# Two-layer graph residual norm on one core: z kept in three h buffers, transposes in other banks, a new order of work on every engine

## The chip, the cores and the metric

The kernel runs on one core of one Trainium2 chip. The metric is the time of one execution on the device, in microseconds; lower is better. The five engines are named PE (TensorE, matmuls; PEld is its loading of weights), DVE (VectorE), ACT (ScalarE), POOL (GpSimd) and SP (SyncE, which here issues all transfers). They run their own instruction streams and meet at semaphores only.

## What is computed

x is 128 batches of 64 nodes with 512 features, fp32. Layer 0 mixes nodes with the squared-by-element adjacency, adds a bias and normalises x plus that. Layer 1 builds two 64 x 64 affinities per batch, from projections z_l and z_g, mixes them, applies them to a value projection, projects again, adds and normalises.

```python
W = support * kernel                                  # layer 0: adj * adj
out = jnp.einsum('bnf,nm->bmf', x, W) + bias
x = _layernorm(x + out, axis=-1)                      # h
z_l = jnp.einsum('bnd,ed->bne', h, W_lang)
z_g = jnp.einsum('bnd,ed->bne', h, W_grav)
v = jnp.einsum('bnd,ed->bne', h, W_V)
A_l = jnp.maximum(jnp.einsum('bnd,bmd->bnm', zn, zn), 0.0) * not_eye      # zn: z_l over its norm
A_g = jnp.exp(-d2 / (2.0 * sigma * sigma)) * not_eye                      # d2: squared distances of z_g
K = w_l * K_l + (1.0 - w_l) * K_g                     # each A times the mask, over its row sums
out = jnp.einsum('bnm,bmd->bnd', K, v)
x = _layernorm(h + jnp.einsum('bnd,ed->bne', out, W_O), axis=-1)
```

## The kernel before

**Tiling.** A pair is two batches, 128 rows; a group is NP = 4 pairs; there are NG = 16 groups. Every fp32 matrix product is made of products of split numbers: hi is the value rounded to fp32r, lo the rest, and three products (hi hi, hi lo, lo hi) are summed. The splitting is two instructions each time: ACT copies a PSUM bank to hi (`hi_proj`, `hi_hT`, `hi_kt`, line 596), then DVE subtracts (`lo_proj` L827, `lo_hT` L821, `lo_kt` L913). Setup turns the four weights into triangular blocks T (so that the Gram product needs only h T h') and into M = W_V' W_O'.

**One group.** `layer0` (L343) makes mix x into bank_x and bank_p; `add_y` (L804) adds the bias into an h buffer, `count_y` (L812, L816) takes mean and variance, POOL's `scale_y` (L1151 to L1156) makes scale and offset, ACT's `normalise_h` (L613) writes h. `transpose_h` (L364) transposes the four pairs, which are split into hT. `project` (L386) makes twelve projections in a ring of three banks: k = 0 to 7 are z parts (3 to 12 matmuls), k = 8 to 11 the values u, one per pair (12 matmuls). `gram` (L408) makes, for half q (two pairs), products of the projections with hT; `copy_q` (ACT) and `sum_q` (POOL, L1186) collect them, `merge` (DVE, L837) adds them to P_sb, `diagonals` (L848, L856) takes the squared norms, POOL's `columns` the inverse norms. `transpose_p` (L422 the matrices into bank_pt, L429 the norms into bank_r) feeds `similarities` (L869 to L880), `exp_g` (ACT, L642), `coefficients` (L890 to L901), `scale_l` (ACT, L647) and `combine` (L907), which writes K. `transpose_k` (L440) transposes K, `apply_k` (L455) multiplies it with u into bank_k and bank_r, `add_z` (L920) adds h and writes to o_sb, `count_z` (L925, L934), POOL's `scale_z` and ACT's `normalise_out` (L656) follow, and SP stores o_sb pair by pair (L320).

**Order.** Nothing is scheduled by a program: `step(g)` on each engine is a list written by hand. In step g, PE takes the projections of group g and, between them, the second half of group g-1 (from `transpose_p` on) and the first part of group g+1 (`layer0`, `transpose_h`). The x of group g+2 is split at the same time (`split_x`, ACT x_hi, POOL x_lo, L1144). Steps 0 and 1 stand alone, a loop takes two steps per pass from 2 to 13, step 14 and a list of its own for group 15 follow. Two h buffers and two hT buffers alternate. Banks are shared: bank_pt holds the transposes 0 and 3 of h, the transposed P and the transposed K; the Gram product of either half uses banks_px (bank_p and bank_x); so each of these waits for the readers of the one before.

**Waits that matter later.** `transpose_h(.., 3)` waits for `hT_split` of pair 0 of the same group; `gram(.., 1)` for `p_merged` of half 0; `transpose_k` for `s2_done` of half 1, so that `similarities` have left bank_pt.

## Time and profile before

| | us |
|---|---|
| runs, median (lowest to highest of 3) | 721.12 (720.65 to 721.17) |
| profiled execution | 719.66 |
| its span, first to last instruction | 717.9 |
| from the first projection of group 1 to that of group 15 (14 steps) | 585.4 |
| one step without low clock | 41.8 |
| group 15 and the end | 56.05 |

The profiled execution's own time is 1.8 us more than its span. Engines are busy 92% (PE), 74% (DVE), 55% (ACT) and 32% (POOL) of the span. The rows of a timeline have the start in us from the span's start, the duration, the engine, the line, and in brackets the engine's idle time before it with what ended it. Names have their buffer numbers left out: banks_kr is bank_k or bank_r, banks_px is bank_p or bank_x. A matmul's record ends after the next one has begun, so durations of PE are not to be summed; starts are to be compared.

### The profile page before, as it was taken

The page shows a single profiled execution, that of the slowest core. Times are in us where ns is not written, and L with a number is a line of the kernel's source. Part 1 is how long each engine was busy: PE and PEld are TensorE (multiplying, and loading weights), DVE is VectorE, ACT ScalarE, POOL GpSimd, SP SyncE. Part 2 cuts the span into 40 slices and gives each one's busy share as a digit, 9 for nine tenths or more (in the row PEclk, how much of TensorE's full clock was granted, in tenths as well). Part 3 has the DMA queues.
Part 4 walks back from the last instruction along what each step waited for, and adds up shares of the span by engine and source line. Part 5 has one row for each costly group of instructions (what it writes and reads, how often), then busy time and mean ns, then how long its engine had stood idle before and what let it go on. Part 6 is the DMA issues. An engine that isn't in the chain of part 4 may idle for free. (4 is left out here: it accounts for less than half of the span.)

```text
span 717.9 us, 11567 instructions
## 1 busy us (share of the span) xinstructions
PE 658.4 (92%) x3323; PEld 545.3 (76%) x3323; DVE 532.0 (74%) x1587; ACT 394.7 (55%) x710; POOL 233.0 (32%) x488
## 2 busy tenths in 40 slices
PE   7999898989989898998989899898989989899874
PEld 7888787778868777787877778787777868788663
DVE  6834885968688596767859676795967679586876
ACT  5645456565645656564555656456564645655533
POOL 1124125151522515152250515225051522503132
PEclk9999999999999999999999999999999999999998
DMA  7210102020110202011020201102020110001002
GB/s 291 77 60 1 58 31 88 24 95 1 60 58 29 88 22 95 0 58 58 29 88 15 102 0 58 58 29 88 14 102 0 58 58 29 29 16 45 0 31 88
DMA packets 20406, 38.32 MB, mean 53 GB/s; under 512 B 1824, under 2 KB 1824, under 8 KB 20384
## 3 DMA queue, kind: packets, MB, share of 16 engines
q1 hardware_dynamic: 20384, 38.05, 14.6%
q8 instruction: 11, 0.18, 0.1%
q14 instruction: 11, 0.09, 0.0%
HBM read 21.27 MB, written 16.78 MB: 53 GB/s over the span
## 5 line engine op out<-in xcount | busy, mean ns | idle before, releaser
L386 PE MATMUL ring<-hT,T_hi 128*128 128x512 f32 x640 | 205.5, 402 | 2.9 <-DVE yT L827 2.9
L386 PEld LDWEIGHTS ring<-hT,T_hi 128*128 128x128 f32 x640 | 115.9, 190 | 30.5 <-DVE yT L827 9.8
L386 PE MATMUL ring<-hT,T_lo 128*128 128x512 f32 x320 | 125.5, 392 | 0.0
L386 PE MATMUL ring<-M_hi,hU 128*128 128x512 f32 x256 | 102.1, 399 | 0.0
L827 DVE TENSOR_TENSOR yT<-ring,yT 128x512 fp32r<-128x512 f32 x128 | 87.3, 682 | 18.9 <-ACT yT L596 18.9
L386 PE MATMUL ring<-M_hi,hT 128*128 128x512 f32 x256 | 100.4, 392 | 0.0
L386 PE MATMUL ring<-M_lo,hU 128*128 128x512 f32 x256 | 100.1, 391 | 0.0
L596 ACT ACTIVATE yT<-ring 128x512 fp32r<-128x512 f32 x128 | 75.1, 587 | 44.5 <-PE ring L386 44.1
L1151 POOL TENSOR_SCALAR z_ve<-z_mv 128x2 f32<-128x2 f32 x32 | 7.0, 218 | 251.0 <-DVE z_mv L934 246.4
L656 ACT ACTIVATE o_sb<-o_sb,z_nb,z_rs 128x512 f32<-128x512 f32 x60 | 47.1, 809 | 73.9 <-POOL z_nb L1156 73.9
L1144 POOL TENSOR_TENSOR x_lo<-x_sb,x_hi 128x512 fp32r<-128x512 f32 x60 | 75.3, 1293 | 22.9 <-ACT x_hi L596 22.9
L408 PE MATMUL banks_px<-yT,hT 128*128 128x256 f32 x496 | 70.8, 300 | 11.8 <-DVE P_sb L837 11.8
L408 PEld LDWEIGHTS banks_px<-yT,hT 128*128 128x128 f32 x496 | 67.1, 204 | 16.5 <-DVE P_sb L837 12.0
L827 DVE TENSOR_TENSOR u_lo<-ring,u_hi 128x512 fp32r<-128x512 f32 x64 | 44.2, 691 | 43.6 <-ACT u_hi L596 43.0
L386 PEld LDWEIGHTS ring<-hT,T_lo 128*128 128x128 f32 x320 | 60.4, 189 | 13.6
L613 ACT ACTIVATE h_sb<-h_sb,y_nb,y_rs 128x512 f32<-128x512 f32 x64 | 48.8, 809 | 26.2 <-POOL y_nb L1156 25.9
L596 ACT ACTIVATE Q_sb<-banks_px 64x512 f32<-64x512 f32 x62 | 36.6, 591 | 46.9 <-PE banks_px L408 46.5
L386 PEld LDWEIGHTS ring<-M_hi,hT 128*128 128x128 f32 x256 | 48.2, 188 | 10.6
L386 PEld LDWEIGHTS ring<-M_lo,hU 128*128 128x128 f32 x256 | 48.4, 189 | 9.9
L386 PEld LDWEIGHTS ring<-M_hi,hU 128*128 128x128 f32 x256 | 48.4, 189 | 9.8
L837 DVE TENSOR_TENSOR P_sb<-banks_px,Q_sum 64x256 f32<-64x256 f32 x62 | 26.2, 422 | 37.8 <-POOL Q_sum L1186 37.0
L821 DVE TENSOR_TENSOR hT<-bank_pt,hT 128x512 fp32r<-128x512 f32 x31 | 21.3, 686 | 40.8 <-ACT hT L596 40.8
(132 smaller groups left out, 1218.5 us busy)
## 6 DMA issues: line engine op xcount, KB each, us to landing
x_sb<-in_x_dram SPq DMA_DIRECT2D x15, 1024.0 KB, 5.3
out_dram<-o_sb SPq DMA_DIRECT2D x60, 256.0 KB, 2.0
x_sb<-in_x_dram SPq DMA_DIRECT2D x2, 512.0 KB, 5.3
w_raw<-in_L_gnn_W_lang_dram SPq DMA_DIRECT2D x1, 1024.0 KB, 6.3
o_sb<-in_L_gnn_W_grav_dram SPq DMA_DIRECT2D x1, 1024.0 KB, 9.1
h_sb<-in_L_gnn_W_V_dram SPq DMA_DIRECT2D x1, 1024.0 KB, 11.3
w_raw<-in_L_gnn_W_O_dram SPq DMA_DIRECT2D x1, 1024.0 KB, 8.0
out_dram<-x_sb SPq DMA_DIRECT2D x4, 256.0 KB, 2.1
```

Source lines behind the costliest of these rows:

```text
L386: last = pe.matmul(bank[:, :], a, b, start=n == 0, stop=n == len(terms) - 1)
L408: last = pe.matmul(q_banks(g, q)[:, pp, b, :, :, :], hT[par][:, i, p, 2 * b:2 * b + 2, :], yT[:, i, :, :, t], start=i == 0, stop=i == DC - 1)
L596: return act.activation(dst, src, ACT.Copy, scale=scale)
L613: act.activation(h_sb[par][:, p, :], h_sb[par][:, p, :], ACT.Identity, scale=y_rs[:, p:p + 1], bias=y_nb[:, p:p + 1]).then_inc(h_ready, 1)
L656: act.activation(out_rows(g)[:, p, :], out_rows(g)[:, p, :], ACT.Identity, scale=z_rs[:, p:p + 1], bias=z_nb[:, p:p + 1]).then_inc(o_ready, 1)
L821: dve.tensor_tensor(hT_lo[par][:, :, p, :, :], hT_bank(g, p).rearrange("p (c b r) -> p c b r", c=DC, b=2), hT_hi[par][:, :, p, :, :], ALU. ...
L827: dve.tensor_tensor(proj_dst(k, 1), ring[ring_of(k)][:, :], proj_dst(k, 0), ALU.subtract).then_inc(proj_split, 1)
L837: last = dve.tensor_tensor(P_sb[q][rows, :, :, rows], q_banks(g, q)[other, :, b, 0, :, :], Q_sum[rows, :, :, :], ALU.add)
L1144: pool.tensor_tensor(x_lo[:, p, :], x_sb[:, p, :], x_hi[:, p, :], ALU.subtract).then_inc(x_lo_done, 1)
L1151: pool.tensor_scalar(ve[:, pq], mv[:, pq, 1], LN_EPS, None, ALU.add).then_inc(ve_done, 1)
```

## The change

- **z in place.** `add_z` writes back to the h buffer, `normalise_out` normalises there and SP stores from there. o_sb is gone; there are three h buffers, `buf = g % 3`. `add_y` waits for the stores of group g-3, `scale_z` for the `normalise_out` of the group before.
- **Banks.** h's transposes go to bank_k, bank_r, bank_k and a ring bank (was bank_pt, bank_k, bank_r, bank_pt); K's go to bank_k (was bank_pt). The waits follow: transpose 2 waits for pair 0's split, transpose 3 for the projection of the ring, the transposed norms and K for hT or z.
- **Order.** Every engine's list is new. PE makes `gram(g, 0)` before projection 9 (was after 10), puts `transpose_p(g, 0)` into step g itself (was in the next step behind projection 0), and takes `transpose_k(g-1, 0)` behind projection 1 (was behind 4), `apply_k` 0 and 1 behind 2, `layer0` behind 3 and 6.
- **Loop.** Since 2 and 3 buffers repeat after 6, the loop of PE, DVE and ACT holds six steps and is passed twice. SP's loads and stores are written out without a loop; POOL's loop holds one step as before.

The core of the diff:

```diff
-        h_sb = [sb(f"h_sb{i}", [R, NP, D]) for i in range(2)]
+        h_sb = [sb(f"h_sb{i}", [R, NP, D]) for i in range(3)]
...
-                                                  for t in (bank_r, bank_x, bank_pt, bank_p)]
+                                                  for t in (bank_r, bank_x, bank_k, bank_p)]
...
-            return (bank_pt, bank_k, bank_r, bank_pt)[p]
+            return (bank_k, bank_r, bank_k, ring[ring_of(0)])[p]
...
-            with sp.Fori(1, NG - 2, 1) as g:
-                load(g + 2)
-                store(g - 1)
-            store(NG - 3)
-            store(NG - 2)
-            store(NG - 1)
+            load(3)
+            for g in range(NG):
+                if g + 4 < NG:
+                    load(g + 4)
+                store(g, g % 3)
...
                 elif p == 3:
 
+                    pe.wait_ge(proj_split, NPROJ * g - NPROJ + 10)
+                elif p == 2:
+
                     pe.wait_ge(hT_split, NP * g + 1)
                 elif isinstance(g, int) and g == 1:
                     pass
-                elif p == 0:
-
-                    pe.wait_ge(kt_split, 2 * g - 2)
                 else:
 
...
-                if q:
+                if not (isinstance(g, int) and g == 0 and q == 0):
                     pe.wait_ge(x0_done, d)
+                if is_last(g):
+                    pass
+                elif q:
+                    pe.wait_ge(z_added, NP * g + 2)
+                else:
+                    pe.wait_ge(hT_split, NP * g + NP + 2)
...
-                if not (isinstance(g, int) and g == NG - 1):
-                    pe.wait_ge(s2_done, 2 * g + 2)
-                if q:
+                if q and is_last(g):
                     pe.wait_ge(kt_split, 2 * g + 1)
+                elif q:
+                    pe.wait_ge(z_added, NP * g + 1)
+                elif not is_last(g):
+                    pe.wait_ge(hT_split, NP * g + NP + 3)
...
-                    pe.wait_ge(x0_done, 2 * g + 2)
+                    pe.wait_ge(x0_done, 2 * g + 1)
                 elif p >= 2:
                     pe.wait_ge(z_added, NP * g + p - 1)
+                if p == 3:
+                    pe.wait_ge(x0_done, 2 * g + 2)
...
-            with pe.Fori(2, NG - 2, 2) as g:
-                step(g, 0)
-                step(g + 1, 1)
-            step(NG - 2, 0)
+            with pe.Fori(2, NG - 2, 6) as g:
+                for i in range(6):
+                    step(g + i, 2 + i)
+            step(NG - 2, NG - 2)
...
-            transpose_p(g - 1, 0)
+            transpose_k(g - 1, 0)
             project(g, 1, 1)
             project(g, 1, 2)
+            apply_k(g - 1, 0)
+            apply_k(g - 1, 1)
             project(g, 1, 3)
             transpose_p(g - 1, 1)
             project(g, 1, 4)
-            transpose_k(g - 1, 0)
             project(g, 1, 5)
             project(g, 1, 6)
-            apply_k(g - 1, 0)
             transpose_k(g - 1, 1)
-            apply_k(g - 1, 1)
             project(g, 1, 7)
             apply_k(g - 1, 2)
             apply_k(g - 1, 3)
             gram(g, 1, 0)
             gram(g, 1, 1)
-
-            pe.wait_ge(kt_split, 2 * g)
-            pe.wait_ge(z_added, NP * g)
+            project(g, 1, 8)
             transpose_p(g, 0)
-            project(g, 1, 8)
+            project(g, 1, 9)
             transpose_p(g, 1)
-            project(g, 1, 9)
             transpose_k(g, 0)
             project(g, 1, 10)
...
+                act.activation(h_sb[buf][:, p, :], h_sb[buf][:, p, :], ACT.Identity, scale=z_rs[:, p:p + 1],
...
             hi_proj(g, 0)
+            scale_l(g - 1, 0)
+            hi_kt(g - 1, 0)
...
-            hi_kt(g - 1, 0)
             scale_l(g - 1, 1)
             hi_proj(g, 5)
             copy_hU(g, 1, 0)
             copy_hU(g, 1, 1)
             hi_proj(g, 6)
+            normalise_out(g - 1, old, 0)
+            normalise_out(g - 1, old, 1)
+            hi_kt(g - 1, 1)
             copy_hU(g, 1, 2)
             copy_hU(g, 1, 3)
-            hi_kt(g - 1, 1)
             hi_proj(g, 7)
             copy_q(g, 0)
-            normalise_out(g - 1, 0)
             copy_q(g, 1)
-            normalise_out(g - 1, 1)
+            hi_proj(g, 8)
             exp_g(g, 0)
-            hi_proj(g, 8)
+            hi_proj(g, 9)
             scale_l(g, 0)
             exp_g(g, 1)
             hi_kt(g, 0)
-            hi_proj(g, 9)
+            hi_proj(g, 10)
             scale_l(g, 1)
             hi_kt(g, 1)
-            hi_proj(g, 10)
+            normalise_out(g - 1, old, 2)
+            normalise_out(g - 1, old, 3)
             hi_proj(g, 11)
-            normalise_out(g - 1, 2)
-            normalise_out(g - 1, 3)
...
+                    if not (isinstance(g, int) and g < 3):
+                        dve.wait_ge(stored[p], 16 * g - 32)
+                    dve.tensor_tensor(h_sb[buf][:, p, :], (bank_x, bank_p)[p % 2][:, :], bias_bc[:, :],
...
+                if not (isinstance(g, int) and g == 0 and q == 0):
+                    dve.wait_ge(kt_done, 2 * g + q)
...
-                if not (isinstance(g, int) and g in (0, NG - 1)):
-                    dve.wait_ge(stored[p], 16 * g)
-                dve.tensor_tensor(out_rows(g)[:, p, :], (bank_k, bank_r)[p % 2][:, :], h_sb[par][:, p, :],
+                dve.tensor_tensor(h_sb[buf][:, p, :], (bank_k, bank_r)[p % 2][:, :], h_sb[buf][:, p, :],
...
-                lo_proj(g, 10)
+                    add_z(g - 1, old, 1)
+                    count_z(g - 1, old, 1)
+                count_y(g + 1, new, 1)
+                merge(g, 0)
+                diagonals(g, 0)
                 lo_hT(g + 1, 1 - par, 0)
                 lo_hT(g + 1, 1 - par, 1)
-                merge(g, 0)
-                lo_proj(g, 11)
+                lo_proj(g, 8)
+                lo_proj(g, 9)
+                similarities(g, 0)
                 lo_hT(g + 1, 1 - par, 2)
                 lo_hT(g + 1, 1 - par, 3)
-                diagonals(g, 0)
+                coefficients(g, 0)
+                lo_proj(g, 10)
+                lo_proj(g, 11)
...
+            lo_proj(g, 0)
+            combine(g - 1, 0)
             merge(g - 1, 1)
             diagonals(g - 1, 1)
-            lo_proj(g, 0)
-            similarities(g - 1, 0)
             lo_proj(g, 1)
-            coefficients(g - 1, 0)
+            lo_kt(g - 1, 0)
             lo_proj(g, 2)
-            combine(g - 1, 0)
...
+                if not (isinstance(g, int) and g == 0):
+                    pool.wait_ge(o_ready, NP * g - NP + 2 * q + 2)
...
+                    scale_z(g - 1, 0)
+                scale_y(g + 1, 0)
                 if ahead:
-                    for p in range(NP):
-                        split_x(g + 2, p)
+                    split_x(g + 2, 0)
+                    split_x(g + 2, 1)
                 sum_q(g, 0)
+                scale_y(g + 1, 1)
                 columns(g, 0)
+                if ahead:
+                    split_x(g + 2, 2)
+                if tail:
+                    scale_z(g - 1, 1)
+                if ahead:
+                    split_x(g + 2, 3)
```

In the rows below x4 means four in a row; ring is one of the three projection banks, ident the identity (a transpose). PE, before, from the last matmul of projection 11 over the end of a step:

```order
L386 MATMUL ring<-M_hi,hT 128x512
L364 MATMUL banks_kr<-ident,h_sb 128x128 x4
L364 MATMUL bank_pt<-ident,h_sb 128x128 x4
L408 MATMUL banks_px<-yT,hT 128x256 x16
L386 MATMUL ring<-hT,T_hi 128x512 x2
L386 MATMUL ring<-hT,T_lo 128x512
```

PE, after, from the last matmul of projection 10, with projection 11 cut; "ring<-ident" is the fourth transpose of h:

```order
L380 MATMUL ring<-M_hi,hT 128x512
L416 MATMUL bank_pt<-ident,P_sb 128x128 x4
L429 MATMUL banks_kr<-ident,inv_norm 128x128 x2
L358 MATMUL banks_kr<-ident,h_sb 128x128 x4
L380 MATMUL ring<-M_hi,hU 128x512
...
L380 MATMUL ring<-M_hi,hT 128x512
L358 MATMUL ring<-ident,h_sb 128x128 x4
L402 MATMUL banks_px<-yT,hT 128x256 x16
L380 MATMUL ring<-hT,T_hi 128x512 x2
```

Nothing behind the fourth transpose changes its place, but it leaves bank_pt for a ring bank and stands alone between projection 11 and the Gram product; the transpose of P and the third transpose of h stand ahead of projection 11.

ACT, before, the end of a step (u_hi are the projections 8 to 11, x_hi the split of x, Q_sb the copies of the Gram products):

```order
L596 ACTIVATE u_hi<-ring 128x512
L656 ACTIVATE o_sb<-o_sb,z_nb,z_rs 128x512
L596 ACTIVATE x_hi<-x_sb 128x1024 x2
L596 ACTIVATE u_hi<-ring 128x512
L596 ACTIVATE Q_sb<-banks_px 64x512 x2
L613 ACTIVATE h_sb<-h_sb,y_nb,y_rs 128x512 x2
L596 ACTIVATE hT<-bank_pt 128x4x2x64
L596 ACTIVATE hT<-banks_kr 128x4x2x64
L596 ACTIVATE u_hi<-ring 128x512
L596 ACTIVATE hT<-banks_kr 128x4x2x64
L596 ACTIVATE hT<-bank_pt 128x4x2x64
```

ACT, after, from the x_hi on:

```order
L595 ACTIVATE x_hi<-x_sb 128x1024
L612 ACTIVATE h_sb<-h_sb,y_nb,y_rs 128x512 x2
L595 ACTIVATE Q_sb<-banks_px 64x512 x2
L595 ACTIVATE x_hi<-x_sb 128x1024
L595 ACTIVATE u_hi<-ring 128x512
L655 ACTIVATE h_sb<-h_sb,z_nb,z_rs 128x512
L595 ACTIVATE u_hi<-ring 128x512
L595 ACTIVATE hT<-banks_kr 128x4x2x64 x2
L612 ACTIVATE h_sb<-h_sb,y_nb,y_rs 128x512
L595 ACTIVATE u_hi<-ring 128x512
L612 ACTIVATE h_sb<-h_sb,y_nb,y_rs 128x512
L655 ACTIVATE h_sb<-h_sb,z_nb,z_rs 128x512
```

The first copy of Q now stands ahead of the second x_hi and of projection 8, and the normalisation of z no longer precedes x_hi.

POOL, before, the end of a step's list:

```order
L1155 ISA
L1156 TENSOR_TENSOR y_nb<-y_nm,y_rs 128x2
L1143 ISA
L1144 TENSOR_TENSOR x_lo<-x_sb,x_hi 128x512 x4
L1182 ISA
L1186 TENSOR_TENSOR Q_sum<-Q_sb 128x256
```

POOL, after:

```order
L1145 TENSOR_TENSOR x_lo<-x_sb,x_hi 128x512 x2
L1185 ISA
L1189 TENSOR_TENSOR Q_sum<-Q_sb 128x256
L1150 REGISTER_ALU
L1152 TENSOR_SCALAR y_ve<-y_mv 128x2
L1154 TENSOR_TENSOR y_rs<-y_ve,pow_neg_half 128x2
L1155 TENSOR_SCALAR y_nm<-y_mv 128x2
```

Q's sum moves ahead of half of the x_lo passes and of one scaling of y.

## Rows read from the trace of the kernel before

**Rows 1.** The page's first part: busy time by engine.

```profile
PE 658.4 (92%) x3323; PEld 545.3 (76%) x3323; DVE 532.0 (74%) x1587; ACT 394.7 (55%) x710; POOL 233.0 (32%) x488
```

**Rows 2.** PE's waits from 76.5 to 661.9 us: total, times, longest.

```profile
PE bank_pt L364 <- DVE hT L821: 16.5, 14, 1.3
PE banks_px L408 <- DVE P_sb L837: 10.9, 14, 0.9
PE bank_pt L440 <- DVE S L869: 8.3, 13, 0.8
PE ring L386 <- DVE yT L827: 2.9, 9, 0.4
```

**Rows 3.** Windows: span, busy PE, PEld, DVE, ACT, POOL, granted clock, DMA share, GB/s.

```profile
76.45:661.85 585.40, 546.65 (x2746) 451.21 (x2745) 445.38 (x1345) 328.96 (x586) 200.26 (x416) 0.99 0.13 47
243.64:285.47 41.83, 38.79 (x198) 31.81 (x197) 31.81 (x99) 23.60 (x42) 14.66 (x30) 1.00 0.14 49
661.85:717.90 56.05, 40.65 (x198) 32.59 (x196) 40.80 (x146) 23.37 (x45) 13.47 (x35) 0.91 0.10 38
448.00:458.00 10.00, 7.97 (x41) 6.84 (x40) 6.27 (x20) 4.46 (x9) 4.29 (x8) 0.83 0.33 105
```

**Rows 4.** Timeline of PE over the end of a step.

```profile
400.66 2.08 PE L408 MATMUL banks_px<-yT,hT 128*128 128x256 f32 x16
402.57 0.60 PE L364 MATMUL bank_pt<-ident,h_sb 128*128 128x128 f32 x4
403.01 0.60 PE L364 MATMUL banks_kr<-ident,h_sb 128*128 128x128 f32 x4
...
405.97 0.40 PE L386 MATMUL ring<-M_hi,hT 128*128 128x512 f32 x1
406.20 0.60 PE L364 MATMUL banks_kr<-ident,h_sb 128*128 128x128 f32 x4
408.04 0.63 PE L364 MATMUL bank_pt<-ident,h_sb 128*128 128x128 f32 x4 [1.23 <-DVE hT L821]
409.43 2.17 PE L408 MATMUL banks_px<-yT,hT 128*128 128x256 f32 x16 [0.77 <-DVE P_sb L837]
```

**Rows 5.** Timelines of ACT and of POOL, one step later.

```profile
443.29 1.99 ACT L596 ACTIVATE x_hi<-x_sb 128x1024 fp32r<-128x1024 f32 x2
...
445.66 1.19 ACT L596 ACTIVATE Q_sb<-banks_px 64x512 f32<-64x512 f32 x2
...
444.41 5.02 POOL L1144 TENSOR_TENSOR x_lo<-x_sb,x_hi 128x512 fp32r<-128x512 f32 x4 [0.34 <-ACT x_hi L596]
449.37 0.74 POOL L1186 TENSOR_TENSOR Q_sum<-Q_sb 128x256 f32<-128x256 f32 x1
```

**Rows 6.** Timeline of DVE: durations of its kinds of work.

```profile
450.37 0.86 DVE L837 TENSOR_TENSOR P_sb<-banks_px,Q_sum 64x256 f32<-64x256 f32 x2
...
426.99 0.61 DVE L907 SCALAR_TENSOR_TENSOR K_sb<-X_g,coef,K_l 128x128 f32<-128x128 f32 x2
...
429.52 1.28 DVE L920 TENSOR_TENSOR o_sb<-banks_kr,h_sb 128x512 f32<-128x512 f32 x2
```

**Rows 7.** PE's waits from 42 to 76.5 us, which is step 0.

```profile
PE banks_px L408 <- DVE P_sb L837: 0.9, 1, 0.9
```

**Rows 8.** DMA queues of the page: packets, MB, share of 16 engines.

```profile
q8 instruction: 11, 0.18, 0.1%
```

**Rows 9.** PE's waits from 661.9 us, the last group.

```profile
PE bank_pt L422 <- DVE P_sb L856: 4.2, 1, 4.2
PE banks_kr L455 <- DVE o_sb L920: 1.1, 1, 1.1
```

**Rows 10.** Timeline of DVE and POOL in the last group.

```profile
689.39 0.29 DVE L848 CUSTOM_DVE_ANT_0 diag_scr<-P_sb,ident 128x128 f32<-128x128 f32 x1
689.40 0.86 POOL L1186 TENSOR_TENSOR Q_sum<-Q_sb 128x256 f32<-128x256 f32 x1 [1.36 <-ACT Q_sb L596]
...
689.60 0.81 DVE L848 CUSTOM_DVE_ANT_0 diag_scr<-P_sb,ident 128x128 f32<-128x128 f32 x1
```

243 lines of the change are left out of this document (113 added, 130 removed).

## Prediction

> **What bounds the kernel now.** Read the page's busy line first: TensorE (PE) is busy 658.4 of 717.9 us, VectorE (DVE) 532.0, ScalarE (ACT) 394.7, GpSimd (POOL) 233.0 [rows 1]. The order in which PE takes its work sets the end, and what PE waits for is the price list. Between 76.5 and 661.9 us, where groups 1 to 14 are projected, PE waits on four lines only: 16.5 us for the fourth transpose of h (14 times), 10.9 before the second Gram product (14), 8.3 before the first transpose of K (13) and 2.9 at projections behind a transpose (9) [rows 2]. That is 38.6 us in 50 waits.
>
> The windows say what a step is: 14 steps take 585.40 us, 41.8 each, with DVE at work for 31.8 us of 41.83, ACT 23.6 and POOL 14.7 [rows 3]. Some steps are longer, those with a stretch of lower granted clock; in the 10 us around such a place it is 0.83 of full speed [rows 3], which is TensorE at its lower level (1.2 GHz) for a third of the stretch: 0.17 x 10 = 1.7 us lost. Four such places (near 160, 327, 453 and 620 us) cost 6.8 us. Two waits of PE stand just before one like it: 1.23 and 0.77 us, 1.4 us apart [rows 4].
>
> A wait costs more than its idle time. Undisturbed, four transposes follow the last four after 0.44 us (402.57 to 403.01); at the wait 1.84 us lie between the starts (406.20 to 408.04), 1.40 more, with 1.23 shown as idle [rows 4]. The other 0.17 is the overlap of neighbouring matmuls, which is lost too. Fifty waits: 50 x 0.17 = 8.5 us. So a step's content is (585.4 - 38.6 - 8.5 - 6.8) / 14 = 531.5 / 14 = 37.96 us. The same from below: 132 matmuls of 512 columns, 0.228 us from start to start, are 30.1; two Gram products of 1.91 are 3.8; 32 transposes of 0.11 are 3.5; 37.4 in all.
>
> **What the change removes.** (1) The fourth transpose of h waited because it and the first one share bank_pt. ACT reached the first copy only after x_hi, a copy of Q and two normalisations, and DVE followed. Now the fourth goes to a ring bank, whose reader is long done, and ACT copies the first two sooner: -16.5 us. (2) The second Gram product waited for merge(g, 0) to read banks_px. In the trace ACT copies Q at 445.66, behind 1.99 us of x_hi, and POOL adds it at 449.37, behind 5.02 us of x_lo, though the Gram product was over near 444.6 [rows 5]. Now the copy stands before the second x_hi, the sum before the last two x_lo, and projection 9, three transposes of h, projection 10, a transpose of P and projection 11 lie between the two Gram products (9 us for a chain of 3.2): -10.9. (3) K's transpose waited for similarities(g, 1) to free bank_pt. It moves to bank_k: -8.3. (4) The 2.9 go with the transposes of P taking another place. With the 8.5 of overlap and, since the pairs of waits are gone, the 6.8 of clock, 14 steps lose 53.9 us and come to 531.5. The clock's share is the uncertain one: it may be 0, which adds 6.8.
>
> **What takes their place.** I laid a step out, from the start S of a group's first projection, with durations from rows: an ACT copy 0.6, a DVE operation of 512 columns 0.68 alone and 0.6 in a row, bn_stats taken as the same, Q's copy 1.20, Q's sum 0.74, merge 0.86, combine 0.61 [rows 5, 6], and 0.05 to 0.15 per handing over. Three places are tight.
>
> First, the four h transposes must be split before S. The fourth one ends 1.9 us before S (the second Gram product lies behind it); then 0.17 until its result is out, 0.6 on ACT, 0.69 on DVE: 1.5. It fits with 0.4 us to spare. Second, projection 11 needs DVE's lo_proj(8), which now stands behind merge, diagonals and two lo_hT: about 1 us to spare. Third, the first transpose of K now stands behind projections 0 and 1 only, 15 matmuls x 0.228 = 3.4 us after S. Its K needs Gram 1: result out 0.17, Q's copy 1.20, sum 0.15 + 0.74, merge 0.05 + 0.86, combine 0.61, two hops 0.1, in all 3.9. **PE waits 0.4 us there**, with the overlap 0.57, in 14 steps: +8.0. From both sides: 0 if hops are nothing, 1.6 (+22 us) if one 0.69 us operation stands in DVE's way and two hops double. I take the walk's value since every part of the chain has a row. Everything else has 0.8 us or more: layer 0 comes later than before, bias adds are done 1.5 us before they are asked for, and DVE has 31.8 us of work for 38.5. ACT has the same count, POOL too. The queue of SP has its loads and stores in the same turn, and h_sb's new wait on `stored` asks for a store of some 17 us before.
>
> Step 0 loses a wait of 0.9 us [rows 7] and its overlap of 0.17, and takes over a transpose of P (0.6): -0.5.
>
> The loop body of PE, DVE and ACT holds six steps instead of two, so it is taken twice, with one jump back instead of five or six. Loading of code shows as 11 packets, 0.18 MB and 0.1% of the engines' time on one queue, about 1 us a packet [rows 8]. The step of 41.83 us shows nothing for a jump; a jump to code that has to be loaded again is not in this trace. Bounds: 0, and 4 us if PE and DVE each wait for two packets in turn. I take +2. The Trainium skill, "Runtime: NRT & Kernel Launch", section on instruction fetch mechanics, says that straight code is prefetched and that a taken branch to a page no longer held stalls; it gives PE room for 2048 instructions, and six steps have 2352 matmuls and weight loads (196 of each in a step). By it the stall comes once per engine, and the page gives no price.
>
> The last group: before, 56.05 us with 4.2, 1.1, 0.8 and 0.8 us of waits [rows 3, 9]. After, laid out in the same way: K's first transpose waits 2.1 us (DVE takes lo_proj(15, 0) before combine); K's second is copied by ACT only behind two normalise_out, which wait for POOL's scale: 3.5; the first Gram 0.5, the transposes of P 0.3 and 0.9, K's first transpose of group 15 3.6 (the big wait of 4.2 moves there), and the last product with K 2.1, because ACT copies projection 11 only behind normalise_out(14, 2) and (3), for which POOL's scale comes late. That is 13.0 against 6.9 before, less 3.2 of low clock (0.09 x 56 = 5.0 before, 1.8 left). +2.9, between -3 and +5.
>
> **Sum.** -53.9 + 8.0 - 0.5 + 2.0 + 2.9 = -41.5. The profiled execution of before took 719.66 us (span 717.9 and 1.8 around it): 719.66 - 41.5 = 678.2. The median of the runs, 721.12, is 1.46 above that execution: **679.6 us**, a step of 38.5 us.
>
> **Rivals.** *DVE is held up at the end of a step.* The new order lets DVE's diagonals(g, 0) run while POOL computes scale_y. At 689.60 one of four equal diagonal operations took 0.81 us instead of 0.29 while POOL's Q_sum ran from 689.40 to 690.26 [rows 10]. Two such clashes a step and one at a seam with only 0.4 us to spare make one more PE wait of 1.2 us: 14 x 1.2 = 17, so 697. Against it: POOL's x_lo passes overlap DVE's work in before too, mostly with operations that read PSUM. The Trainium skill, "SBUF — State Buffer", section on two separate sides, has a rule that speaks against this change: GpSimd and a DVE operation with two SBUF inputs exclude each other for a whole instruction. The row at 689.60 agrees with it. 20%.
>
> *Code loading shows at every packet.* The code of before is some six and a half steps long (setup, 0, 1, two in the loop, 14 and the last group), with 11 packets on the queue, 1.7 a step. If the twelve loop steps each had to load theirs, visibly at 1 us, that is +20, so 700. Against: step 0 is code taken for the first time in before too, and PE's waits there are 1 us in all, on DVE [rows 7]. 4%.
>
> *Slower.* ACT must take normalise_out(g-1, 2) and (3) before and after Q's second copy; they wait for POOL's scale_z(g-1, 1), which stands behind Q's sum, scale_y, columns and one x_lo: 7.0 us of POOL in a row (0.9, 1.6, 1.6, 1.3 and 1.6 with the hops), done 3.1 us before ACT asks. If that stretch took twice as long (14.0), ACT would copy Q late by 3.9, and K's transpose would wait 4.3 us instead of 0.4: 14 x (37.96 + 4.5) = 594, against 585.4 now; +9, and with +4.4 of the other terms (-0.5 + 2.0 + 2.9) the result is 734. It becomes slower than before once POOL's stretch is 6.4 us longer. For it: POOL's order is fixed. Against: POOL works 14.7 us in a step. 5%.
>
> *The order is changed but the wait only moves* by its full 3.4 us a step, because DVE's order is the true limit: 721, no change. DVE's idle time (10 us a step) speaks against it. 2%.
>
> **Chances and range.** Forecast 69% (669 to 690: K's wait 0 to 1.0 us, clock back or not, last group -3 to +5), DVE held up 20% (690 to 702), code 4%, slower 5%, moved wait 2%. The range 668 to 699 takes in the forecast's own and most of the second case; about 2 in 10 lie outside. About 0.2% is what a measurement of this kernel can tell from no change; faster by more than that 94%, within 1%, slower 5%.
>
> **What the profile would show.** PE's waits at the fourth h transpose and at Gram 1 gone, one wait of about 0.4 us at K's first transpose in each step; steps of 38.5 us; granted clock 1.00 from 5 us to the last group; DVE's busy share near 80%; in the last group the longest wait at K's transposes. The forecast is wrong if PE waits at a group's first projection (the h seam had nothing to spare), if POOL's or DVE's mean durations rise, or if one step in the middle of the loop is longer by more than 4 us (the jump).

## The result, and the profile after

The changed kernel took 681.51 us (median; 681.27 to 682.10 in 4 runs) beside 720.88 us for the kernel before (719.97 to 721.17, 4 runs). The ratio is 0.9457, with a 95% interval of 0.9441 to 0.9473: faster by 5.4%. The forecast was 679.6 us in a range of 668 to 699. The profiled execution has a span of 679.5 us; the forecast for it, 678.2 less the 1.8 around the span, was 676.4.

| us | before | forecast | after |
|---|---|---|---|
| start to group 1's first projection | 76.45 | 75.95 | 75.44 |
| 14 steps | 585.4 | 541.5 | 538.2 |
| one step in the loop | 41.83 | 38.5 | 38.15 |
| group 15 and the end | 56.05 | 58.9 | 65.8 |
| span | 717.9 | 676.4 | 679.5 |

The page of after, busy time by engine, and the queue that loads code (packets, MB, share); compare [rows 1, 8]:

```profile
PE 647.1 (95%) x3323; PEld 543.3 (80%) x3323; DVE 535.7 (79%) x1587; ACT 396.2 (58%) x710; POOL 237.4 (35%) x488
...
q8 instruction: 30, 0.49, 0.3%
```

PE's waits in after, first over the 14 steps (75.4 to 613.6 us; compare [rows 2]), then behind them (compare [rows 9]): total, times, longest.

```profile
PE banks_kr L442 <- DVE K_sb L913: 4.6, 13, 0.4
PE ring L380 <- issue: 2.9, 1, 2.9
```

```profile
PE banks_kr L459 <- DVE KT_lo L919: 3.8, 1, 3.8
PE banks_px L442 <- DVE K_sb L913: 3.2, 2, 2.6
PE banks_kr L442 <- DVE K_sb L913: 2.0, 1, 2.0
PE bank_pt L416 <- DVE S L873: 1.9, 1, 1.9
PE banks_kr L459 <- issue: 1.7, 1, 1.7
```

Fifty waits of 38.6 us have become fourteen of 7.5 us: one of 0.37 us in 13 of the steps at K's first transpose, and one that nothing in the profile ends. The windows of after (columns as in [rows 3]): the 14 steps, one step, and group 15 with the end.

```profile
75.44:613.67 538.23, 530.70 (x2747) 445.72 (x2746) 449.20 (x1346) 329.78 (x585) 204.92 (x416) 1.00 0.15 51
232.60:270.80 38.20, 37.83 (x198) 31.80 (x197) 32.12 (x96) 23.80 (x44) 15.00 (x30) 1.00 0.18 57
...
613.67:679.50 65.83, 44.66 (x192) 35.14 (x190) 38.87 (x131) 23.89 (x46) 11.84 (x31) 0.83 0.11 41
```

The end of a step on PE in after, which answers to [rows 4]. The fourth transpose goes to a ring bank and Gram 1 starts 0.35 us behind it; the only idle time comes at K's transpose.

```profile
420.77 0.60 PE L358 MATMUL ring<-ident,h_sb 128*128 128x128 f32 x4
421.12 2.15 PE L402 MATMUL banks_px<-yT,hT 128*128 128x256 f32 x16
423.11 0.63 PE L380 MATMUL ring<-hT,T_hi 128*128 128x512 f32 x2
...
426.31 0.39 PE L380 MATMUL ring<-hT,T_lo 128*128 128x512 f32 x1
427.07 0.43 PE L442 MATMUL banks_kr<-ident,K_sb 128*128 128x128 f32 x2 [0.37 <-DVE K_sb L913]
```

### The profile page after: what moved, and what is told of

Same layout as the page of the kernel before. It is cut to its first block and busy times, and to the rows that moved or that the text cites. A ratio compares the mean times of both kernels' runs of the same rounds, so it can differ in the third digit from the quotient of the medians.

```text
span 679.5 us, 11318 instructions
## 1 busy us (share of the span) xinstructions
PE 647.1 (95%) x3323; PEld 543.3 (80%) x3323; DVE 535.7 (79%) x1587; ACT 396.2 (58%) x710; POOL 237.4 (35%) x488
## 5 line engine op out<-in xcount | busy, mean ns | idle before, releaser
L380 PE MATMUL ring<-hT,T_hi 128*128 128x512 f32 x640 | 203.2, 399 | 2.9 <-issue 2.9
L380 PEld LDWEIGHTS ring<-hT,T_hi 128*128 128x128 f32 x640 | 118.2, 190 | 26.1 <-issue 3.1
L831 DVE TENSOR_TENSOR yT<-ring,yT 128x512 fp32r<-128x512 f32 x128 | 83.5, 680 | 12.9 <-ACT yT L595 12.9
L380 PEld LDWEIGHTS ring<-hT,T_lo 128*128 128x128 f32 x320 | 60.8, 190 | 13.5
L402 PE MATMUL banks_px<-yT,hT 128*128 128x256 f32 x496 | 67.0, 289 | 0.0
L402 PEld LDWEIGHTS banks_px<-yT,hT 128*128 128x128 f32 x496 | 64.0, 195 | 1.4
L1189 POOL TENSOR_TENSOR Q_sum<-Q_sb 128x256 f32<-128x256 f32 x32 | 23.6, 738 | 112.8 <-ACT Q_sb L595 112.8
L923 DVE TENSOR_TENSOR h_sb<-banks_kr,h_sb 128x512 f32<-128x512 f32 x64 | 43.6, 690 | 19.7 <-PE banks_kr L459 19.7
L655 ACT ACTIVATE h_sb<-h_sb,z_nb,z_rs 128x512 f32<-128x512 f32 x63 | 50.8, 811 | 9.4 <-POOL z_nb L1157 9.0
L1152 POOL TENSOR_SCALAR y_ve<-y_mv 128x2 f32<-128x2 f32 x32 | 7.3, 228 | 136.3 <-DVE y_mv L820 135.1
L595 ACT ACTIVATE u_hi<-ring 128x512 fp32r<-128x512 f32 x64 | 37.9, 594 | 16.0 <-PE ring L380 15.6
```

The costliest lines, as they stand in the source:

```text
L380: last = pe.matmul(bank[:, :], a, b, start=n == 0, stop=n == len(terms) - 1)
L402: last = pe.matmul(q_banks(g, q)[:, pp, b, :, :, :], hT[par][:, i, p, 2 * b:2 * b + 2, :], yT[:, i, :, :, t], start=i == 0, stop=i == DC - 1)
L595: return act.activation(dst, src, ACT.Copy, scale=scale)
L655: act.activation(h_sb[buf][:, p, :], h_sb[buf][:, p, :], ACT.Identity, scale=z_rs[:, p:p + 1], bias=z_nb[:, p:p + 1]).then_inc(o_ready, 1)
L831: dve.tensor_tensor(proj_dst(k, 1), ring[ring_of(k)][:, :], proj_dst(k, 0), ALU.subtract).then_inc(proj_split, 1)
L923: dve.tensor_tensor(h_sb[buf][:, p, :], (bank_k, bank_r)[p % 2][:, :], h_sb[buf][:, p, :], ALU.add).then_inc(z_added, 1)
```

## Experiments

Eleven kernels ran. The fourth column is the difference of medians to the kernel named, 681.5 for the changed one and 720.6, 720.2 or 719.6 for the one before in the three sets; the intervals are those of the ratio to before. The last columns come from each kernel's profiled execution. The changed kernel was not run again beside them, and by the width of the intervals a difference to it is known to some 1.5 us.

| kernel | median | ratio to before, 95% | difference | 14 steps | group 15, end |
|---|---|---|---|---|---|
| e1_no_jump | 675.56 | 0.9355 to 0.9393 | -6.0 to after | 532.8 | 66.2 |
| e11_pe_no_jump | 682.19 | 0.9458 to 0.9489 | +0.7 to after | 539.9 | 65.8 |
| e2_before_six_steps | 724.59 | 1.0040 to 1.0084 | +4.0 to before | 588.1 | 57.0 |
| e10_before_four_steps | 727.07 | 1.0079 to 1.0113 | +7.5 to before | 592.3 | 56.9 |
| e3_before_banks_only | 721.98 | 1.0007 to 1.0033 | +1.4 to before | 585.5 | 57.2 |
| e4_after_old_banks | 679.89 | 0.9427 to 0.9461 | -1.6 to after | 537.5 | 63.4 |
| e5_grams_order_before | 678.94 | 0.9407 to 0.9438 | -2.6 to after | 535.5 | 66.6 |
| e9_sum_merge_early | 704.52 | 0.9772 to 0.9805 | -15.1 to before | 570.7 | 57.0 |
| e7_k_transpose_later | 675.27 | 0.9346 to 0.9395 | -6.2 to after | 531.1 | 66.5 |
| e6_last_group_order | 673.15 | 0.9337 to 0.9368 | -8.4 to after | 538.1 | 57.2 |
| e8_all_three | 656.32 | 0.9101 to 0.9132 | -25.2 to after | 526.3 | 52.8 |

### Banks or order

Two kernels take banks and order apart. The first puts the new banks into the kernel before; beside the line shown it moves K's transposes to bank_k, fits the semaphores that are waited for, and in the last group lets two operations change places on PE and on DVE:

```diff
-            return (bank_pt, bank_k, bank_r, bank_pt)[p]
+            return (bank_k, bank_r, bank_k, ring[ring_of(0)])[p]
```

> The kernel before with the change's banks alone: the four hT groups go to bank_k, bank_r, bank_k and a bank of the ring, K's transposes to bank_k, and the order of all engines stays (but in the last group, where two operations change places so that a bank is free). It tells what the banks do by themselves. In the kernel before the fourth h transpose waited 16.5 us in all for DVE's K_lo, and K's first transpose 8.3 us for DVE's h split 3, both of them places in bank_pt. Theory (the banks are a condition of the new order, not the gain): K_lo still comes late in DVE's order, so the wait for it moves to Gram 1 or to K's transposes of the next step, and the time falls by less than a third of the gain: 708 to 721. Rival (the banks are the gain, the order only fits them): both waits go, 721 - 16.5 - 8.3 = 696, or less with the clock that is given back.

It took 721.98 us, by its interval 0.1 to 0.3% more than before. PE's waits over its 14 steps, and their window:

```profile
PE banks_kr L364 <- DVE hT L821: 16.5, 14, 1.3
PE banks_kr L440 <- DVE o_sb L920: 10.1, 14, 0.8
PE banks_px L408 <- DVE P_sb L837: 4.8, 14, 0.4
PE ring L386 <- DVE yT L827: 4.5, 13, 0.4
PE banks_kr L455 <- DVE KT_lo L913: 1.6, 8, 0.2
```

```profile
76.37:661.89 585.52, 547.27 (x2747) 443.36 (x2745) 445.56 (x1345) 328.50 (x586) 200.28 (x416) 1.00 0.13 47
```

The 16.5 us are there to the tenth; only the place differs: now the third transpose of h waits, for DVE to read what the first one left in bank_k. K's transpose waits 10.1 us for `add_z` instead of 8.3 for `similarities`. (The expectation names the readers of before wrongly; [rows 2] have DVE's split of hT at the fourth transpose and `similarities` at K's.) Freeing a bank saved nothing, since the reader of the bank was late, not the bank scarce.

The second keeps the changed kernel's order and gives back the old bank:

```diff
-            return (bank_k, bank_r, bank_k, ring[ring_of(0)])[p]
+            return (bank_k, bank_r, bank_k, bank_pt)[p]
...
-                                                  for t in (bank_r, bank_x, bank_k, bank_p)]
+                                                  for t in (bank_r, bank_x, bank_pt, bank_p)]
```

> The changed kernel, its new order on every engine, with K's transposes and the fourth h transpose put back in bank_pt; the waits on semaphores are those that this bank asks for. Theory (in the new order DVE's K_lo is done long before the fourth h transpose asks for the bank, and its h split 3 long before K's transposes do): 681.5, within 0.7 us, with no PE wait at the fourth h transpose. Rival (the banks carry the gain): the waits of the kernel before come back at the fourth h transpose, 1.2 us a step, and at K's first transpose: 695 to 705.

It took 679.89 us, with a step of 38.07 us (38.15 in after) and no wait at the fourth transpose. Its interval overlaps that of after, so the -1.6 us is not told from nothing. In this order bank_pt would do as well as the new banks for these two transposes: the banks do not carry the gain. What is left is the order together with the third h buffer, and no run takes these two apart.

### What removed the wait at Gram 1

> The changed kernel with one piece of the old order back on two engines: ACT copies Q behind both of its x_hi splits, and POOL takes the sum for Q behind all four x_lo passes instead of between them. PE's own order stays, in which 9 us of h transposes stand between Gram 0 and Gram 1. Theory (the Gram 1 wait of the kernel before, 10.9 us in all, went because PE now takes Gram 0 that much earlier, not because ACT or POOL moved): the same 681.5, within 1 us. Rival (ACT's and POOL's place of that work did it): a wait of about 0.8 us a step comes back at Gram 1 or at K's transposes, 681.5 + 11 = 692.

```diff
 ACT
-                copy_q(g, 0)
...
+                copy_q(g, 0)
 POOL
-                    split_x(g + 2, 0)
-                    split_x(g + 2, 1)
+                    for p in range(NP):
+                        split_x(g + 2, p)
                 sum_q(g, 0)
```

Putting ACT's and POOL's old place of this work back into the changed kernel cost nothing: a step of 38.13 us, and the same waits over the 14 steps but one.

```profile
PE banks_kr L442 <- DVE K_sb L913: 4.5, 13, 0.4
PE ring L380 <- DVE u_lo L831: 1.8, 1, 1.8
```

The second row is what the jump left here, 1.8 us instead of 2.9, with no low clock behind it. The two steps around the jump take 40.12 + 38.01 = 78.13 us in this trace and 41.22 + 39.52 = 80.74 in after; the 2.6 between them is the whole difference of the medians. DVE's stop at the jump (below) is 2.3 us here:

```profile
346.66 0.86 DVE L841 TENSOR_TENSOR P_sb<-banks_px,Q_sum 64x256 f32<-64x256 f32 x2 [2.31 <-issue]
```

Why it is shorter than after's 4.9 is not settled. It also takes the total outside the 1 us that the theory allowed.

The counterpart moves POOL and DVE in the kernel before and leaves PE and ACT:

```diff
 POOL
                 if ahead:
-                    for p in range(NP):
+                    for p in range(2):
                         split_x(g + 2, p)
                 sum_q(g, 0)
+                if ahead:
+                    for p in range(2, NP):
+                        split_x(g + 2, p)
 DVE
+                merge(g, 0)
                 lo_hT(g + 1, 1 - par, 0)
                 lo_hT(g + 1, 1 - par, 1)
-                merge(g, 0)
```

> The kernel before with two edits of order: POOL takes the sum for Q behind two of its four x_lo passes (was behind all four, 2.6 us later), and DVE takes merge(g, 0) ahead of the splits of hT 0 and 1 (was behind them, while it waits 2.6 us for ACT's hT). PE and ACT keep their order. In the trace of before Q is copied at 446.84, the sum runs from 449.37, the merge from 450.37, and Gram 1 starts 0.77 late in this step (10.9 us in all). Theory (Gram 1's wait hangs on POOL's and DVE's place of this work and not on PE's place of Gram 0): it goes, 721 - 10.9 = 710, and the wait of 1.2 us at the fourth h transpose stays. Rival (with PE's order as before the wait only moves, to the fourth h transpose or to the next projection): 716 to 721. With experiment e5, which put ACT's and POOL's order back in the changed kernel at no cost, it tells whether one engine or any of them could have removed this wait.

This gave more than either theory: 704.52 us, 15.1 less. By the traces the steps lost 14.7: 7.7 of waits (38.6 to 30.9), and 7.0 that no wait shows, with ten waits fewer and no low clock in the steps (both are estimated further down). PE's waits over the 14 steps and their window:

```profile
PE bank_pt L364 <- DVE hT L821: 16.5, 14, 1.3
PE bank_pt L440 <- DVE S L869: 10.6, 14, 0.8
PE ring L386 <- DVE yT L827: 3.8, 12, 0.4
```

```profile
75.10:645.83 570.73, 539.63 (x2747) 445.11 (x2745) 443.99 (x1347) 328.61 (x586) 200.46 (x416) 1.00 0.14 50
```

POOL's and DVE's timelines at the end of a step show the sum between the x_lo passes and the merge in the place where DVE used to stand idle (compare [rows 5]):

```profile
434.83 2.55 POOL L1144 TENSOR_TENSOR x_lo<-x_sb,x_hi 128x512 fp32r<-128x512 f32 x2 [0.35 <-ACT x_hi L596]
437.34 0.75 POOL L1186 TENSOR_TENSOR Q_sum<-Q_sb 128x256 f32<-128x256 f32 x1
```

```profile
438.21 0.86 DVE L837 TENSOR_TENSOR P_sb<-banks_px,Q_sum 64x256 f32<-64x256 f32 x2 [1.31 <-POOL Q_sum L1186]
439.47 0.69 DVE L821 TENSOR_TENSOR hT<-bank_pt,hT 128x512 fp32r<-128x512 f32 x1 [0.40 <-ACT hT L596]
```

Gram 1's wait is gone with PE's order untouched, so PE's new order is not needed for it; by e5, ACT's and POOL's new places are not needed once PE has its new order. One thing is common to after, e5 and e9: DVE takes the merge ahead of the splits of hT. No run takes that back, so whether PE's order alone would have been enough is not shown. Two edits of order carry 15.1 of the 39.4 us between the two kernels. The rest of the gain, among it the wait of the fourth transpose, was not split further: it needs h earlier, and so ACT's, DVE's and POOL's lists together.

### The jump

> The changed kernel with the loops of PE, DVE and ACT written out, so that no engine jumps back between step 7 and step 8; the order of the work is the same. In the changed kernel PE waited 2.9 us at 345 us, at the first projection of step 8, with nothing that the profile shows to release it, and 3.4 us of the granted clock at half followed (about 1.7 us lost in them). Theory (the jump back into code that is no longer held costs this): the wait and the low clock are gone, 681.5 - 4.4 = 677. Rival (the place is slow for another reason, a wait of step 7's end, or a chunk of code that comes late wherever it stands): the same 681.5, and a PE wait of about 3 us at step 8 stays. A third way (code written out loads more packets in all and shows them elsewhere): 681 to 684, with new PE waits.

> The changed kernel with PE's loop alone written out; DVE and ACT keep their loop and their jump back. With all three written out the time fell from 681.5 to 675.6. Theory (PE's own jump costs, since PE is the bound and its wait has no releaser; the others' jumps fall in their idle time): 675.5 to 677, and the 2.9 us wait is gone. Rival (DVE's or ACT's jump would hold PE up by itself): 678 to 681, with a PE wait of 1 to 3 us for DVE or ACT at about 345 us.

```diff
-            with pe.Fori(2, NG - 2, 6) as g:
+            for g in range(2, NG - 2, 6):
```

The same line stands on ACT and DVE; e1 changes all three, e11 PE's alone. In after, all three engines stop at the same place for something that the profile does not show:

```profile
345.43 0.72 PE L380 MATMUL ring<-hT,T_hi 128*128 128x512 f32 x2 [2.91 <-issue]
```

```profile
348.32 0.69 ACT L646 ACTIVATE K_l<-X_l,coef 128x128 f32<-128x128 f32 x2 [3.73 <-issue]
```

```profile
349.14 0.86 DVE L841 TENSOR_TENSOR P_sb<-banks_px,Q_sum 64x256 f32<-64x256 f32 x2 [4.92 <-issue]
```

With all three written out the time fell by 6.0 us, to 675.56. The two steps around the jump cost 80.74 - 2 x 38.15 = 4.4 us in after, and each step of e1 is 0.08 us shorter, about 1.1 in 14. The latter is no price of the jump: most steps of e4 and e11, which jump, are as short (38.07 and 38.08 us). With PE's alone written out nothing was gained: PE no longer stopped, ran on, and met DVE's stop at K's transpose. The first row is PE's only wait between 340 and 360 us in e11, the second DVE's timeline there.

```profile
PE banks_kr L442 <- DVE K_sb L913: 5.0, 1, 5.0
```

```profile
348.92 0.86 DVE L841 TENSOR_TENSOR P_sb<-banks_px,Q_sum 64x256 f32<-64x256 f32 x2 [5.13 <-issue]
```

So the theory of e11, that the jumps of the others fall into their idle time, fell; its rival was right in kind, with a longer wait than it had put. The stops lie side by side, and DVE's ends last (no kernel writes out DVE's loop alone): in after, PE resumed at 345.43, lost some time to low clock and had K_sb ready when it came to it; in e4 it resumed as late with no low clock and waited 1.6 us for K_sb, and the two steps took 41.31 + 39.44 = 80.75 us, as in after. In e11 a longer stretch of low clock (348.5 to 355.4 us) followed the wait, and they took 38.07 + 45.04 = 83.1.

How long may a body be? Two kernels change the loop of the kernel before, on PE, ACT and DVE, and nothing else. The edit of e10 on PE; e2 has 6 in place of 4:

```diff
-            with pe.Fori(2, NG - 2, 2) as g:
-                step(g, 0)
-                step(g + 1, 1)
+            with pe.Fori(2, NG - 2, 4) as g:
+                for i in range(4):
+                    step(g + i, i % 2)
```

> The kernel before with a loop body of six steps in place of two: the order of every engine is untouched, and there is one jump back in place of five. Theory (a jump back of two steps is free, one of six steps costs what the changed kernel shows, 2.9 us of PE wait and some low clock, and loading four more steps of code is hidden): 721 + 3 to 5 = 724 to 726. Rival 1 (the long body costs nothing of itself, and the changed kernel's wait comes from its own order): 721. Rival 2 (the code of every step that is newly loaded costs something): over 728.

> The kernel before with a loop body of four steps in place of two, so with two jumps back, before steps 6 and 10, in place of five. The body of six cost +4.0 us for its one jump. Theory A (four steps of code are already too much to be held, so each jump costs what that one did): 720.6 + 2 x 4 = 729, with PE waits of about 3 us, ended by nothing that the profile shows, at steps 6 and 10. Theory B (four steps are still held, as two are): 720.6, with no such wait. Between them (part of the code is still there): 722 to 726.

Six steps (one jump) cost 4.0 us, four steps (two jumps) 7.5, 3.7 each. The 7.5 lie between theory A (8) and the case between, and the trace has theory A's stops at both jumps. In e2 PE stopped twice, 1.9 us at 373 and 1.4 us at 376 us; the row is of e10, PE's waits of that kind between 280 and 500 us (total, times, longest):

```profile
PE ring L386 <- issue: 7.2, 2, 3.7
```

Code is loaded on q8 and on q14. From 200 to 600 us, inside the loop, before has neither queue in its list of queues, only the data's; e10 has both (packets, MB, share):

```profile
q1 hardware_dynamic: 10391, 19.78, 13.9%
```

```profile
q8 instruction: 20, 0.33, 0.4%
q14 instruction: 14, 0.11, 0.1%
```

So a body of two steps is held and loads nothing, one of four is loaded over and over, and a jump back into code that is no longer held stops PE for 1.9 us or more (e2, e10). The Trainium skill, "Runtime: NRT & Kernel Launch", section on instruction fetch mechanics, says that a taken branch outside the window held stalls until the page has come; the trace agrees and gives the price. The room of 2048 instructions that the Trainium skill gives PE in the same section is not borne out as a bound for a loop: four steps are 1568 matmuls and weight loads, some 1730 with the waits and register instructions that the trace of e10 shows, and PE stopped. q8 carried 27 packets in e1 and 30 in after, with no wait of PE in e1's steps but K's: straight code is loaded unseen.

### The wait that the steps have left

> The changed kernel with K's first transpose one projection later in every step (behind projection 2, with DVE's and ACT's lists fitted to it). The changed kernel waits 0.37 us a step there, for DVE's K_sb. Theory (this wait is the only one that the steps have left, and the projections stay covered): it goes, and with it the gap beside it, 14 x 0.37 = 5.2 to 14 x 0.54 = 7.6 us less: 674 to 676. Rival (with K later, apply_k and the layer behind it ask DVE or ACT for their operands sooner than these are done): a wait of the same size stands at apply_k or at the fourth projection, 681 to 684, and above 684 if it is over 0.6 us a step.

```diff
 PE
+                project(g, par, 2)
                 if tail:
                     transpose_k(g - 1, 0)
-                project(g, par, 2)
+                project(g, par, 3)
 ...
-                project(g, par, 3)
```

It took 675.27 us, 6.2 less. Over the steps PE's waits are down to the jump:

```profile
PE ring L380 <- issue: 2.8, 1, 2.8
```

A step without any wait takes 37.57 us. One projection of cover was enough for the chain that the forecast walked (Q's copy, sum, merge, combine), and nothing behind it came late.

### The last group

> The changed kernel with the first part of the last group in the order of the steps: K's first transpose behind projection 1, DVE's merge and combine first, ACT's scale_l and hi_kt first, and the output of group 14 normalised behind hi_kt(1). In the changed kernel PE waited 2.0 us at K's first transpose in the last group and 3.8 us at apply_k, and half-clock stretches of 3.4 and 6.8 us stood behind them. Theory (the waits come from DVE's and ACT's order there, and the low clock from the waits): the two waits fall to 0.4 us and 0.3 us (-5.1), and the low clock behind them mostly goes (up to -4): 672 to 676.5. Rival 1 (the low clock is the last group's own and does not hang on these waits): -5, so 676.5, with half-clock stretches as long as before. Rival 2 (the waits move to transposes of P or to the second half of the group): 680 to 682.

```diff
 PE
-            transpose_k(g - 1, 0)
             project(g, 1, 1)
+            transpose_k(g - 1, 0)
 ACT
-            hi_proj(g, 0)
             scale_l(g - 1, 0)
             hi_kt(g - 1, 0)
+            hi_proj(g, 0)
 ...
-            normalise_out(g - 1, old, 0)
-            normalise_out(g - 1, old, 1)
 ...
+            normalise_out(g - 1, old, 0)
+            normalise_out(g - 1, old, 1)
 DVE
-            lo_proj(g, 0)
-            combine(g - 1, 0)
             merge(g - 1, 1)
+            combine(g - 1, 0)
```

The two waits fell from 2.0 to 0.2 and from 3.8 to 1.3, 4.3 us together, yet the time fell by 8.4 to 673.15. PE's two waits from 613.6 us on (the other rows, of 3.2, 1.9 and 1.7 us, are as in after), and the windows of the whole and of its part up to 648.8:

```profile
...
PE banks_kr L459 <- DVE KT_lo L919: 1.3, 1, 1.3
PE banks_kr L442 <- DVE K_sb L913: 0.2, 1, 0.2
```

```profile
613.63:670.80 57.17, 40.36 (x192) 31.61 (x190) 38.67 (x131) 23.71 (x46) 11.81 (x31) 0.90 0.12 47
613.63:648.80 35.17, 29.50 (x152) 23.57 (x150) 26.72 (x96) 17.43 (x35) 7.78 (x19) 1.00 0.08 31
```

In after, the place behind the 3.8 us wait reads otherwise:

```profile
637.00:643.90 6.90, 6.22 (x23) 5.65 (x24) 2.46 (x4) 1.68 (x4) 0.00 (x0) 0.51 0.20 76
```

That is PE at its lower level (1.2 GHz) for 6.9 us; nothing like it stands in e6 ahead of 648.9 us. Up to PE's last matmul after has 13.7 us at half clock in this group (3.4 at 620.0, 6.8 at 637.0, 3.4 at 657.5), e6 3.4. The other 4 us of the gain are then mostly this clock (the overlap that two waits lose is 0.7 at most), and Rival 1 falls. But the waits do not fix the clock by themselves: e4 has the waits of after in this group, only 6.8 us at half clock, and 63.4 us in place of 65.8. Against e4, e6 is 6.2 us shorter for 4.5 us of waits. A wait here was paid between one and a half times and twice.

### All of it

> Three edits of the changed kernel together: loops written out, K's first transpose behind projection 2, the last group's first part in the order of the steps, and new for this kernel, in the second half of the last group, projections of the last outputs between K's transposes so that these wait less. Theory (the parts add up): 681.5 - 4.4 (jump) - 5 to -7.6 (K's wait) - 5 to -9 (first part of the last group) - 2 to -3 (its second part) = 658 to 665. Rival (they do not add, since PE that comes earlier meets DVE or ACT at the next seam; DVE is busy 79% already): 666 to 674, with PE waits at places that have none in the changed kernel.

To e1, e6 and e7 together this kernel adds, in the second half of group 15, projections between K's transposes, with ACT's and DVE's lists fitted to it:

```diff
 PE, group 15
-            transpose_k(g, 0)
             project(g, 1, 10)
+            transpose_k(g, 0)
+            project(g, 1, 11)
+            transpose_k(g, 1)
             apply_k(g, 0)
             apply_k(g, 1)
-            transpose_k(g, 1)
-            project(g, 1, 11)
```

It took 656.32 us: 8.8% less than before, 25.2 less than after, and below the range that the theory gave. The three parts measured by themselves add up to 20.6 (6.0 + 6.2 + 8.4); 4.6 are left for the new one. Windows of the 14 steps and of the last group, and PE's waits in the latter; over the 14 steps there are none.

```profile
75.39:601.71 526.32, 526.30 (x2747) 444.62 (x2746) 447.28 (x1346) 333.00 (x585) 205.35 (x416) 1.00 0.16 52
...
601.71:654.50 52.79, 40.01 (x192) 31.81 (x190) 38.45 (x131) 23.61 (x46) 11.81 (x31) 0.93 0.13 50
```

```profile
PE bank_pt L416 <- DVE S L874: 1.9, 1, 1.9
PE banks_kr L459 <- DVE KT_lo L920: 0.9, 1, 0.9
PE banks_kr L459 <- DVE h_sb L924: 0.8, 1, 0.8
PE banks_kr L442 <- DVE K_sb L914: 0.2, 1, 0.2
```

PE is now busy for the whole of 526.32 us. In the steps no idle time of PE is left for an order to take.

## Why the prediction was right, and where its terms were off

The mechanism held in the steps: the waits of [rows 2] went, and one new wait came where the walk had put it, at 0.37 us against 0.4 forecast. In the last group four of the walk's waits stood at their place and size (2.0 against 2.1 us, 3.8 against 3.5, 3.2 in two against 3.6, 1.7 against 2.1); the transposes of P had one of 1.9 in place of 0.3 and 0.9, the Gram product none in place of 0.5 (12.6 us in all against 13.0). The terms, one by one:

- **What was removed from the steps: 53.9 forecast, 59.1 measured.** A step's content was put at 37.96 us; e8, whose steps have no wait, shows 526.3 / 14 = 37.6 (the forecast's own sum from below, 37.4, was nearer). Two figures were off, in opposite ways. *The overlap lost per wait* was 0.17. The start behind a wait does come 0.16 us later than its idle time says, in e3 as in after. But the old order loses more than that: at full clock e3 has 585.5 - 526.3 - 37.5 of waits = 21.7 us for 63 waits, and e9 570.7 - 526.3 - 30.9 = 13.5 for 40, a mean of 0.34. The next start but one is up to 0.1 us late too, and some starts are late with no idle time shown (two by 0.1 us at 252.5 and 252.9 us in e3, behind the transposed norms). By this mean fifty waits are 17.0, not 8.5. *The clock* was 6.8; by the same estimate 585.4 - 526.3 - 38.6 - 17.0 = 3.5 are left for it in before. e3 shows why it is less: it ran its 14 steps at full clock and took 585.5 us, as long as before with its four low stretches. The steps of before with a low stretch are 42.9 to 43.4 us long and those right behind them 39.6 to 40.9, against 41.8: the first three such pairs take 83.6, 84.0 and 83.8 us, two undisturbed steps 83.8. With PE late its next waits are shorter, and here that gave all of it back.
- **K's wait: +8.0 forecast, 7.5 measured** (538.2 - 526.3 - 4.4 for the jump). A step of after is 0.58 us longer than one of e7: 0.37 of idle time and 0.21 beside it, where the forecast had 0.17.
- **The jump: +2.0 forecast, 4.4 measured.** The upper bound had been put at 4 for two packets in turn on PE and DVE; the engines stop 2.9 to 4.9 us each, side by side, and the longest, DVE's, ends last.
- **Step 0: -0.5 forecast**, -1.0 by the start of the first step.
- **The last group: +2.9 forecast, +9.8 measured.** This is the term that failed. The sum of its waits was right, +6.1 forecast and +5.7 measured; its clock was not. The forecast let the clock improve, from 5.0 us lost to 1.8 (-3.2), though the same walk had put seven waits of 0.3 to 3.6 us there. Most of the 5.0 could not come back: behind 709.35 us before has no matmul, and the low clock there (the second row) costs PE nothing. Up to there it had one stretch of 3.4 us, 1.7 lost.

```profile
661.85:709.35 47.50, 40.65 (x198) 32.59 (x196) 37.83 (x138) 21.04 (x42) 10.78 (x27) 0.96 0.03 13
709.40:717.86 8.46, 0.00 (x0) 0.00 (x0) 2.92 (x9) 2.33 (x3) 2.69 (x8) 0.62 0.45 175
```

The window of after has a clock of 0.83, so 0.17 x 65.8 = 11.2 us lost, of which the last 8.3 us have no matmul and count for 4.2: 7 us that PE paid, some 5 more than before where 3.2 less was forecast. e6 shows the tie to the waits: waits less by 4.3, time less by 8.4; e4 shows that with the same waits it can be 2.4 us less.

That the total came so near is in part luck: the errors partly cancel (-3.3 in the steps, +6.9 in the last group, -0.5 at the start: +3.1 in the span), and the median came 1.9 us above the forecast. One sign of being wrong came in a small size: POOL's mean duration in the steps rose from 0.481 to 0.493 us and DVE's from 0.331 to 0.334, with no wait of PE behind it.

Two readings of the prediction were right in size and wrong in their reason. Point (1) put 16.5 us down to bank_pt, point (3) 8.3 us to the bank of K: e3 shows that the banks alone are worth nothing, and e4 that bank_pt can be given back. Point (2) put 10.9 us down to three moves at once; e9 removes the wait without PE's, e5 without ACT's and POOL's.

*The rivals.* DVE held up by POOL did not come: over after's whole run the diagonals took the same time, where before had one of 0.8 us. The rows are the operation's ns, lowest, median and highest, of before and of after:

```profile
L848 DVE CUSTOM_DVE_ANT_0 diag_scr<-P_sb,ident x128: 280/285/805, 76.1 to 693.8; 128x128 f32<-128x128 f32 x128
```

```profile
L852 DVE CUSTOM_DVE_ANT_0 diag_scr<-P_sb,ident x128: 283/287/294, 66.0 to 652.1; 128x128 f32<-128x128 f32 x128
```

Diagonals did run beside POOL's scalings of y, as the rival had it, but those are operations on 128x2 elements and left them at 294 ns at most; the 805 ns of before came beside Q_sum, a 128x256 one, and in after no diagonal meets it. The rule of the Trainium skill ("SBUF — State Buffer", section on two separate sides) was therefore hardly tested on long operations here; one X_l of DVE (L884) that started at 71.14 us, while POOL's x_lo ran, took 378 ns instead of 290, which agrees with it. The case drawn from the rule had the right pair of engines and the wrong POOL operation. Code loading did not show at each packet: 30 packets, one stop. The slower case needed POOL's stretch twice as long; POOL is busy 237.4 us against 233.0. That the wait only moves is refused by 38.15 us a step.

## What to carry to other kernels

When an engine waits for a shared bank, ask first when its last reader could have been done: another bank moves the wait (e3), an earlier reader removes it (e9, two edits for 15 us), and once the order is right the bank hardly matters (e4). Count a wait by its idle time and what is lost beside it (0.21 us at K's transpose in after, 0.34 on average in e3 and e9), and in a tail with several waits by the clock too, where it was worth up to as much again (e6, e4). Of low clock in the tail count only what lies ahead of the last matmul. A loop body that outgrows what the engines hold cost 4 us a jump; the buffers' period should not decide its length without that being counted, and writing the loop out on PE alone gained nothing (e11).

## What the runs showed of the hardware that was not expected

- A jump back in a loop of two steps shows no stop on any engine and no code is loaded in the loop (no packet on q8 or q14 from 200 to 600 us in before). In a loop of four or six, code is loaded all along (20 and 14 packets in e10) and PE stops for 1.4 to 3.7 us; in after DVE stops for 4.9 and ACT for 3.7 at the same time, in e5 for 2.3 and 1.4, and PE waits 1.8 there. Four steps are 1568 matmuls and weight loads on PE.
- Four stretches of half clock, 3.4 us each, did not lengthen the steps of before, where 6.8 us had been counted: the first three pairs of steps that hold one take 83.6 to 84.0 us, undisturbed ones 83.8, because the next waits became shorter.
- A wait of PE costs more than the idle time that the profile gives it: 0.16 us at the start behind it, 0.21 in all at K's transpose in after, and on average 0.34 in the order of before (e3 and e9).
- One DVE operation with both inputs in SBUF that starts while a long POOL operation runs ends behind it (one case in each kernel): 805 ns instead of 285 beside Q_sum (before), 378 instead of 290 beside x_lo (after), and at most 294 beside POOL's operations on 128x2.
